# Query and key stacks of a decoder layer: two of four head groups moved within SBUF instead of through DRAM

## The reference, cut to what matters

```python
q = heads(hidden_states @ Wq)
k = heads(hidden_states @ Wk)
v = heads(hidden_states @ Wv)
scores = jnp.einsum('bhqd,bhkd->bhqk', q, k) / jnp.sqrt(jnp.float32(D))
attn = jax.nn.softmax(scores, axis=-1)
std = jnp.einsum('bhqk,bhkd->bhqd', attn, v)
```

## Time and profile before

| | us |
|---|---|
| runs of the kernel before: 1515.85, 1517.29, 1525.48; median | 1517.29 |
| profiled execution, its own time | 1519.1 |
| span of the profiled execution, first to last instruction | 1516.6 |
| DVE busy | 1245.1 (82%) |
| PE busy | 1194.1 (79%) |
| ACT busy | 759.7 (50%) |
| GpSimd busy | 214.6 (14%) |

### The profile page before, as it was taken

One profiled execution on the slowest core, in us unless ns is written; L12 is line 12 of the kernel. 1 busy time (PEld: TensorE's weight loads), 2 busy tenths in 40 slices (PEclk: granted clock), 3 DMA queues, 4 the chain that ended last, 5 costly groups with the idle time before them and its releaser, 6 DMA issues.

```text
span 1516.6 us, 14134 instructions
## 1 busy us (share of the span) xinstructions
PE 1194.1 (79%) x4565; PEld 560.5 (37%) x4570; DVE 1245.1 (82%) x1485; ACT 759.7 (50%) x1110; POOL 214.6 (14%) x247
## 2 busy tenths in 40 slices
PE   4673748677788987887988797887898887887896
PEld 3342313222244542332344443333344533333453
DVE  5877988988879998778789997888889996887434
ACT  6765434435366643636566632555476633552231
POOL 1000122001111123200111122101111132001101
PEclk8755978888879998979989998899799998888898
DMA  6853687456338869544239869434159777452132
GB/s 190 273 174 121 146 213 181 104 119 139 65 100 210 240 145 221 144 113 98 64 91 235 220 159 239 105 85 111 50 143 248 171 195 194 98 129 59 49 98 69
DMA packets 113688, 220.17 MB, mean 145 GB/s; under 512 B 15584, under 2 KB 26336, under 8 KB 113616
## 3 DMA queue, kind: packets, MB, share of 16 engines
q1 hardware_dynamic: 94240, 151.25, 33.8%
q0 software_dynamic: 18432, 67.12, 23.0%
q10 hardware_dynamic: 944, 0.92, 0.2%
HBM read 122.37 MB, written 29.62 MB: 100 GB/s over the span
## 4 chain that ended last, share of the span: by engine, by line
DVE 39%; PE 30%; issue 10%; ACT 5%; DMA 4%; POOL 1%; SPq 1%; DVEq 0%; ACTq 0%; POOLq 0%
DVE ST L876 14%; DVE ST L868 6%; PE ps L1467 5%; PE ps L1285 5%; DVE MX L932 5%; PE ps L1268 4%; PE ps L1420 3%; PE ps L1349 2%; PE ps L1436 2%; DVE ST L879 2%; PE ps L1377 2%; DVE RD L1081 2%; DVE QAK L1096 2%; DMA qk_parts<-PT 2%; PE ps L1236 1%
## 5 line engine op out<-in xcount | busy, mean ns | idle before, releaser
L876 DVE TENSOR_TENSOR_SCAN ST<-dA,ST 128x1024 f32<-128x1024 f32 x128 | 312.6, 2442 | 8.8 <-ACT dA L579 6.0
L1467 PE MATMUL ps<-V,GU 128*128 128x512 f16 x1024 | 240.3, 390 | 5.6 <-DVE V L1063 5.6
L473 POOL DMA_DIRECT2D YA<-ST x128 | 111.0, 867 | 945.0 <-DVE ST L879 887.0
L932 DVE TENSOR_REDUCE MX<-ps 128x1 f32<-128x512 f32 x256 | 165.1, 686 | 84.7 <-PE ps L1268 84.0
L579 ACT ACTIVATE dA<-DL,Aneg 128x511 f32<-128x511 f32 x256 | 168.4, 713 | 82.4 <-DVE ST L876 82.1
L711 ACT ACTIVATE PT<-ps 128x1024 f32<-128x1024 f32 x128 | 126.3, 1021 | 119.0 <-PE ps L1377 118.2
L1268 PE MATMUL ps<-KS,QS 96*128 96x512 f32 x256 | 127.6, 560 | 74.1 <-DVE MX L932 42.3
L1436 PE MATMUL ps<-WP,QS 128*128 128x512 f32 x512 | 144.8, 427 | 29.5 <-DMA WP<-proj_tiles 21.7
L879 DVE TENSOR_TENSOR ST<-ST,BC 128x1024 f32<-128x1024 f32 x128 | 159.4, 1246 | 4.4
L868 DVE TENSOR_TENSOR ST<-DU,BC 128x1024 f32<-128x1024 f32 x128 | 155.8, 1217 | 7.3 <-DMA BC<-bc_rows 7.3
L1467 PEld LDWEIGHTS ps<-V,GU 128*128 128x128 bf16 x1024 | 97.6, 100 | 136.5 <-issue 27.3
(11 more groups left out here) (230 smaller groups left out, 1593.9 us busy)
## 6 DMA issues: line engine op xcount, KB each, us to landing
YA<-ST POOLq DMA_DIRECT2D x128, 512.0 KB, 7.2
BC<-bc_rows SPq DMA_DIRECT2D x64, 512.0 KB, 6.1
qk_parts<-PT SPq DMA_DIRECT2D x64, 256.0 KB, 4.3
GU<-gu_tiles SPq DMA_DIRECT2D x64, 256.0 KB, 8.5
WP<-proj_tiles SPq DMA_DIRECT2D x64, 256.0 KB, 7.3
QS<-qk_parts SPq DMA_DIRECT2D x96, 128.0 KB, 3.4
KS<-qk_parts SPq DMA_DIRECT2D x96, 128.0 KB, 3.8
ST<-in_L_ffn_w_gate_up_dram SPq DMA_DIRECT2D x16, 256.0 KB, 3.4
```

Of the source, the lines that this page charges most:

```text
L876: nc.vector.tensor_tensor_scan(flat, dA[:, a, :, :].rearrange("p e s -> p (e s)"), flat, 0.0, ALU.mult, ALU.add).then_inc(s_scan, 1)
L932: nc.vector.tensor_reduce(MX[:, j % 2, qt, h:h + 1], ps[:, n % 2, :], AX_X, ALU.max).then_inc(s_mx, 1)
L1467: last = mm(ps[:, f % F_RING, :], GU[:, t % GU_RING, k, m * P:(m + 1) * P], XHL[:, z, k, :], start=(k == 0 and z == 0), stop=(k == KT - 1 ...
```

## The change

The parts of units 0 to 3 (groups 0 and 1) are no longer written to DRAM. SP copies each of them out of `QKP` straight into the stacks: one transfer per head and row block, 32 partitions of 2 KB. A high part goes to two row blocks (8 transfers), a low part to one (4). `load_stack` remains for groups 2 and 3. The waits for a free `QKP` buffer go to the stacks' semaphores for these units (`wait_unit_moved`), and the counts of `s_stack` and `s_part` change with it: 288 a batch in place of 192, and 64 in place of 128. In the first batch SP waits ahead of unit 1 for the last ternary weights to have been stored from a buffer that lies in the stacks' memory; before, it did so ahead of the stack of group 1.

```diff
--- before.py
+++ after.py
@@ -276,6 +276,21 @@
         X_AHEAD = X_CHUNK[0][0]
         KV_GROUP = NG - 2
         X_FIRST = [0, 0, 4, 10, 16]
+        HI_ROWS, LO_ROWS = ((0, 1), (0, 2)), ((2,), (1,))
+
+        def stack_filled(b, j):
+
+            return 288 * b + (192 if j < 2 else 288)
+
+        def wait_unit_moved(engine, b, u):
+
+            j, z = UNITS[u]
+            if j < 2:
+                for pair in range(HG // 2):
+                    engine.wait_ge(s_stack[j][pair], 288 * b + 96 * (z + 1))
+            else:
+                engine.wait_ge(s_part[u % 2], 64 * b + 32 * (u // 2 - 1))
+
         ROWS1 = (2, 3, 0, 1)
         UNITS = ((0, 0), (1, 0), (0, 1), (1, 1), (2, 0), (3, 0), (2, 1), (3, 1))
 
@@ -339,19 +354,21 @@
             def load_stack(b, j):
 
                 i = j % 2
-                if j >= 2:
-                    sp.wait_ge(s_s, 2 * KT * NG * b + 2 * KT * (j - 1))
-                else:
-
-                    sp.wait_ge(s_part[j], 32 * KT * b + 64)
-                    if j == 1 and type(b) is int and b == 0:
-                        sp.wait_ge(s_wst[1], 16 * NT)
+                sp.wait_ge(s_s, 2 * KT * NG * b + 2 * KT * (j - 1))
                 for pair in range(HG // 2):
                     first_row = P * j + 2 * D * pair
                     for r, (zq, zk) in enumerate(((0, 0), (0, 1), (1, 0))):
                         for z, dst, part in ((0, QS[i], zq), (1, KS[i], zk)):
                             src = qk_parts[b, z, part, first_row:first_row + 2 * D, :].rearrange("(h p) s -> p h s", p=D)
                             sp.dma_start(dst[D * r:D * r + D, 2 * pair:2 * pair + 2, :].bitcast(F32), src).then_inc(s_stack[i][pair], 16)
+
+            def move_part(u, part, rows):
+
+                j, z = UNITS[u]
+                for h in range(HG):
+                    for r in rows[z]:
+                        sp.dma_start((QS, KS)[z][j][D * r:D * r + D, h, :].bitcast(F32),
+                                     QKP[D * h:D * h + D, 2 * part + u % 2, :].bitcast(F32)).then_inc(s_stack[j][h // 2], 16)
 
             def load_next_bc(b, halves):
                 for n, a in halves:
@@ -365,12 +382,18 @@
                 for r in range(2 * KT):
                     load_next_bc(b, fill_halves(r, first))
                 for u, (j, z) in enumerate(UNITS):
+                    if b == 0 and u == 1:
+                        sp.wait_ge(s_wst[1], 16 * NT)
                     sp.wait_ge(s_hi, 2 * NG * b + u + 1)
-                    sp.dma_start(qk_parts[b, z, 0, P * j:P * j + P, :], QKP[:, u % 2, :].bitcast(F32)).then_inc(s_part[u % 2], 16)
+                    if j < 2:
+                        move_part(u, 0, HI_ROWS)
+                    else:
+                        sp.dma_start(qk_parts[b, z, 0, P * j:P * j + P, :], QKP[:, u % 2, :].bitcast(F32)).then_inc(s_part[u % 2], 16)
                     sp.wait_ge(s_lo, 2 * NG * b + u + 1)
-                    sp.dma_start(qk_parts[b, z, 1, P * j:P * j + P, :], QKP[:, 2 + u % 2, :].bitcast(F32)).then_inc(s_part[u % 2], 16)
-                    if u in (2, 3):
-                        load_stack(b, j)
+                    if j < 2:
+                        move_part(u, 1, LO_ROWS)
+                    else:
+                        sp.dma_start(qk_parts[b, z, 1, P * j:P * j + P, :], QKP[:, 2 + u % 2, :].bitcast(F32)).then_inc(s_part[u % 2], 16)
                     load_next_bc(b, fill_halves(2 * KT + u, first))
                 for j in range(NG + 1):
                     for c, chunk in enumerate(slot_halves(j, first)):
@@ -483,7 +506,7 @@
                 def low_part(u):
                     pool.wait_ge(s_hi, 2 * NG * b + u + 1)
                     if u >= 2:
-                        pool.wait_ge(s_part[u % 2], 32 * KT * b + 32 * (u // 2))
+                        wait_unit_moved(pool, b, u - 2)
                     nc.gpsimd.tensor_tensor(QKP[:, 2 + u % 2, :], PT[:, 0, u % 2, :], QKP[:, u % 2, :].bitcast(F32),
                                             ALU.subtract).then_inc(s_lo, 1)
 
@@ -671,7 +694,7 @@
                     nc.scalar.copy(PT[:, 0, u % 2, :], bank)
                     nc.scalar.square(PT[:, 0, 2 + u % 2, :], bank).then_inc(s_q32, 1)
                     if u >= 2:
-                        act.wait_ge(s_part[u % 2], 32 * KT * b + 32 * (u // 2))
+                        wait_unit_moved(act, b, u - 2)
                     nc.scalar.copy(QKP[:, u % 2, :], bank).then_inc(s_hi, 1)
                     for n, a in fill_halves(2 * KT + u, first):
                         exp_dA(b, n, a)
@@ -705,8 +728,8 @@
                                 act.wait_ge(s_lo, 2 * NG * (b + 1))
                             else:
 
-                                act.wait_ge(s_part[0], 32 * KT * (b + 1))
-                                act.wait_ge(s_part[1], 32 * KT * (b + 1))
+                                act.wait_ge(s_part[0], 64 * (b + 1))
+                                act.wait_ge(s_part[1], 64 * (b + 1))
                             bank = score_bank(b, j, 2 * p)
                             nc.scalar.activation(PT[:, kt % 2, 2 * p:2 * p + 2, :], ps[:, bank:bank + 2, :],
                                                  ACT.Exp, scale=SCALE).then_inc(s_exp, 1)
@@ -1258,7 +1281,7 @@
                     n = 16 * j + m
                     h, qt = m // KT, m % KT
                     if m % (2 * KT) == 0:
-                        pe.wait_ge(s_stack[i][h // 2], 96 * (2 * b + j // 2 + 1))
+                        pe.wait_ge(s_stack[i][h // 2], stack_filled(b, j))
                     if n >= 2:
                         pe.wait_ge(s_mx, 16 * NG * b + n - 1)
                     if j > 0 and m == 0:
```

## The result

The changed kernel takes 1558.78 us (median of 4 runs, 1552.02 to 1561.36) where the kernel before, run beside it, takes 1518.35 (1515.85 to 1525.48): a ratio of 1.0251, 95% interval 1.022 to 1.0281. It is slower by 2.5%. The prediction, 1517.1 us and no change, was wrong, and the time lies outside its range. The profiled executions differ by 33.4 us in their spans (1516.6 and 1550.0); that of the kernel after is its fastest of the four, the medians differ by 40.4.

A forecast was written before the change was run, and what follows sets the result against it. DVE (82% busy) and TensorE (79%) bound the kernel, so only waits could change: 1519.1 - 5.6 (first batch) + 5.4 (three later batches) = 1518.9, as median 1517.1 us, no change; range 1507 to 1530.

The forecast's parts named there:

- the term 24 x 0.46: Fill stage, SP's list: the 24 moves of units 1 and 2 at 0.46 us each take 11.0 us.
- the upper bound, 0.69: SP's time per move at most 0.69 us, the mean of twelve last-batch DRAM loads with the DMA engines full.
- the predicted lateness of the scan, 2.8 us: Batches two to four: the fill stage's last scan starts 16.3 us after unit 1's mark, not 13.45; net 1.8 a batch.
- landing: Time for a move to arrive in the stack: 3.4 us, with 2.0 and 9.9 as ends.
- The chain: Batches two to four: 24 moves, landing, unit 4's cast and exponentials, then the stage's last scan; 16.3 us together.
- Rival 2: SP held back in the saturated stretch, 0.69 us a move, scan 8.3 us late: 1535.2 us; chance 0.16.
- breakeven of 0.46: Rival 2's time per move i where 3 x (24 i + 5.23 - 13.45 - 1.0) passes the first batch's saved 5.6 us.
- Rival 1: Moves faster than the late scan needs, 12.7 us under 13.45; only the first batch counts: 1511.7 us; chance 0.20.
- First batch, predicted -5.6: State 6's B/C load issued at 204.1, not 212.78: DVE's 6.8 us wait goes, 1.2 come back, gain 5.6 us.
- Rival 3: First batch: B/C load issued early, but the stage after it takes the 5.6 us back: 1522.7 us; chance 0.14.

The follow-up runs named there:

- group 0 alone: Changed kernel, but only head group 0 (units 0 and 2) moved within SBUF, group 1 through DRAM as before: 1536.22 us, ratio 1.008 to 1.013.
- Half the bytes: Changed kernel with as many moves, each carrying 256 of the 512 columns (32 KB), the other columns left out: 1553.66 us, ratio 1.018 to 1.026.
- half the moves: Changed kernel with 24 moves a batch, heads 0 and 2 only, 64 KB each, the other heads left out: 1523.22 us, ratio 0.999 to 1.002.

## Why the prediction was wrong, step by step

**The step that failed is the term 24 x 0.46.** It took the issue of a move from loads out of DRAM. A move within SBUF holds SP for 0.59 us, with its gap 0.63, and with the stalls 24 of them take 18.9 us (1265.78 to 1284.68) where 11.0 were put: 4.1 us more for the dearer issue (24 x 0.63 = 15.1), 3.8 for the stalls. The price of the issue could have been read: the trace of the kernel before has one kind of transfer within SBUF, the bias row, 8 KB, issued by ACT. That line (least, median, most in ns):

```profile
L630 ACTq DMA_DIRECT2D QS<-XD x16: 580/588/1182, 251.9 to 1350.7; - x16
```

It was passed over for loads of a nearer size and destination. The nearest row was the one with the same two ends, not the one with the same bytes. The stalls could have been read too: the upper bound, 0.69, is the cheaper issue with stalls, so the two had to be added, not chosen between.

**A smaller term was left out:** unit 0's twelve moves. They hold unit 1 back: it starts 12.4 us after unit 0's first transfer (1253.40 to 1265.78), before 9.4 (1230.28 to 1239.67). Part of these 3.0 us is the B/C load between the two units, whose issue took 1.44 us here and 0.37 before. In the last batch the predicted lateness of the scan, 2.8 us, thus becomes 2.8 + 7.9 (24 moves) + 3.0 (unit 0) - 1.9 (landing: 1.5 from the last issue's end to the cast, where 3.4 was put) = 11.8, and the scan itself is 1.2 shorter: the 10.6 us measured.

**What held.** The chain was the right one: cast of unit 4, exponentials behind it, late scan, shorter scan. DVE was the one to wait, as said, and neither landing nor bytes set the limit. Rival 2 had the mechanism and the sign; its 0.69 a move was too low. Its own formula at 0.79 gives 24 x 0.79 + 5.23 - 13.45 - 1.0 = 9.7 us a batch. Its breakeven of 0.46 was the warning: the value chosen lay just on it. (Rival 1's 1514 for 0.46 and a landing of 2.0 is 1513.0 by that formula; nothing hangs on it.)

**First batch, predicted -5.6: measured -0.1.** The same two terms: unit 1 began at 195.07 behind unit 0's moves, not at 193.03, and units 1 and 2 took 19.0 us, so the load came at 214.14. With 24 moves in all, or group 0 alone, the gain is there at the first maxima, 5.6 and 6.1 us. Rival 3 said that the stage behind would take it back. In the kernel before with the B/C load put first that is what happened, at the next B/C load; in the kernel after there was nothing to take back.

**The rules weighed.** The profile shows a unit's twelve moves holding SP for 7.6 to 12 us while one lands in 3.2. The Trainium skill (DMA: Bandwidth & Descriptors, section Issuing engines are not separate DMA queues) calls the time to start a transfer usually small beside the transfer; the prediction noted the disagreement and still priced it too low. Half the bytes and 1 KB a move left the issue at 0.59 us. The limit of the ports for transfers on 32 partitions (the Trainium skill, SBUF — State Buffer, section Door 1: The DMA port swizzle) was therefore not what set the issue's time. The median landing went from 3.2 us to 2.5 with half the bytes and to 2.3 with 1 KB; no run here isolates the ports' part in that.

## What to carry to other kernels

In these runs a transfer has a price on the engine that issues it, 0.59 us within SBUF at 1, 32 and 64 KB alike. Before a few large ones become many small ones, multiply the count by the issue time of the row with the same kind of source and destination, and add the stalls that such rows show. Then look what stands behind them in that engine's list, and which in-order engine waits on a buffer that they must empty. Where a gain depends on one wait that goes, look for the next load in the same list: here an earlier load by 8.5 us was worth nothing in the end.

## What the runs showed of the hardware

- An issue on SP within SBUF took 0.59 us in the median at 1, 32 and 64 KB, one on ACT 0.59 at 8 KB; with DRAM as the source 0.42 to 0.43 at 64 and 128 KB.
- In the kernel after some nine of the last batch's 48 moves took 1 to 2 us; such ones are there with 1 KB a move too. They don't go with the bytes. They go with GpSimd's accumulations: 32 of the 33 such moves of the four batches begin while one is under way; what makes them so is not shown. The loads from DRAM in the kernel before had some too (1.40 and 1.28 us in a row, at 1254.34 and 1255.78).
- POOL issued moves at 0.5 us each, where its 512 KB accumulations show 0.87.
- TensorE's products of one line (four of L1326 with half the moves, at 1282.40; four of L1302 in the kernel before, at 1278.16) took 1.92 us at a granted clock of 0.50, that is 1.2 GHz, and 1.03 at 1.00, 2.4 GHz. With half the moves TensorE had been busy throughout the 8 us to 1278, at 1.00, before the clock fell.
